# A transformer layer's prologue rearranged: quarter inputs, fewer fills, a resident bias table, another scratch layout

## The reference

```python
# setup: x (2, 1024, 128); D = 128, 16 heads of 8, F = 512; f32
def _L0_attn_ref(x, Wq, bq, Wk, bk, Wv, bv, Wo, bo, rel_emb):
    ...
    q = (x @ Wq.T + bq).reshape(b, n, h, hd).transpose(0, 2, 1, 3)   # k, v alike
    ...
    sim = jnp.einsum('bhid,bhjd->bhij', q, k)
    rp_bucket = _rel_pos_bucket_causal(n)        # 32 buckets of i - j, log spaced up to 128
    bias = rel_emb[rp_bucket]
    sim = sim + jnp.transpose(bias, (2, 0, 1)) * SCALE
    ...
    sim = sim + causal
    attn = jax.nn.softmax(sim, axis=-1)
    out = jnp.einsum('bhij,bhjd->bhid', attn, v)
    out = out.transpose(0, 2, 1, 3).reshape(b, n, d)
    return out @ Wo.T + bo

def _L0_ffn_ref(tgt, router_w, router_b, w1, b1, w2, b2, gamma, beta):
    ...
    rw = jnp.zeros_like(rw).at[..., 0].set(1.0)  # only expert 0 counts
    h = jax.nn.relu(jnp.einsum('bsd,edf->besf', tgt, w1) + b1[None, :, None, :])
    eo = jnp.einsum('besf,efd->besd', h, w2) + b2[None, :, None, :]
    tgt2 = jnp.einsum('besd,bse->bsd', eo, rw)
    x = tgt + tgt2
    ...
    return (x - mean) * jax.lax.rsqrt(var + LN_EPS) * gamma + beta

x = x + _L0_attn_ref(_layernorm(x), ...)
x = x + _L0_ffn_ref(_layernorm(x), ...)
```

## Time and profile before

| | us |
|---|---|
| median of 3 runs | 405.28 (403.5 to 411.39) |
| the profiled execution | 402.29 |
| its span on the core | 400.5 |

### The profile page before, as it was taken

The page is one execution under the profiler, slowest core; times in us unless marked ns, Lnnn a source line. Parts: engine busy times, 40 slices in busy tenths (PEclk is TensorE's granted clock), DMA queues, the critical chain, the costliest instruction groups (busy, mean ns, idle before and its releaser), DMA issues.

```text
span 400.5 us, 8158 instructions
## 1 busy us (share of the span) xinstructions
PE 321.0 (80%) x3197; PEld 153.1 (38%) x3197; DVE 287.5 (72%) x960; ACT 184.0 (46%) x258; POOL 69.5 (17%) x78
## 2 busy tenths in 40 slices
PE   0182438396999899799889979988988998999982
PEld 0131215143334335334434433443443344337752
DVE  3985356358668589588678848967875996773986
ACT  1042024131655554575565545556555545873330
POOL 9812035700001000100100100010010000161552
PEclk9996586668699999999999989999998999999998
DMA  8013422410012101201201220331222010100011
GB/s 227 26 53 116 145 90 95 148 64 3 2 43 66 39 18 52 81 1 61 75 12 44 68 64 2 86 88 26 65 79 55 15 16 12 33 2 10 5 52 53
DMA packets 18295, 21.97 MB, mean 55 GB/s; under 512 B 5584, under 2 KB 14960, under 8 KB 18256
## 3 DMA queue, kind: packets, MB, share of 16 engines
q1 hardware_dynamic: 18256, 21.45, 18.5%
HBM read 14.98 MB, written 4.23 MB: 48 GB/s over the span
## 4 chain that ended last, share of the span: by engine, by line
PE 51%; DVE 17%; DMA 15%; ACT 7%; issue 5%; SPq 4%; POOL 1%; DVEq 0%; POOLq 0%; ACTq 0%
PE ps L1015 14%; PE ps L1044 13%; PE ps L1001 13%; DMA QA<-mrow 7%; ACT PT L626 6%; PE ps L1032 5%; DMA qk_scratch<-QS 4%; DVE FM L759 3%; DVE XN L701 2%; DVE junk L766 2%; DMA KA<-qk_scratch 2%; DMA rows<-in_vectors 2%; PE ps L1077 2%; DVE st L836 1%; DVE U L889 1%
## 5 line engine op out<-in xcount | busy, mean ns | idle before, releaser
L626 ACT ACTIVATE PT<-ps 128x1024 f32<-128x1024 f32 (+1 forms) x192 | 145.8, 810 | 132.4 <-PE ps L1032 101.9
L759 DVE TENSOR_REDUCE FM<-ps 128x1 f32<-128x512 f32 (+3 forms) x176 | 108.4, 660 | 29.2 <-PE ps L1001 29.1
L1001 PE MATMUL ps<-KA,QA 96*128 96x256 bf16 (+3 forms) x544 | 108.7, 294 | 17.6 <-DMA KA<-qk_scratch 14.3
L1015 PE MATMUL ps<-QA,KA 98*128 98x512 bf16 (+3 forms) x384 | 99.0, 343 | 25.4 <-DMA QA<-mrow 10.3
L766 DVE CUSTOM_DVE_ANT_0 junk<-ps,NB 128x256 bf16<-128x256 f32 (+1 forms) x224 | 78.8, 403 | 37.3 <-PE ps L1001 37.2
L1044 PE MATMUL ps<-PT,VG 128*16 128x512 f32 (+3 forms) x768 | 86.9, 498 | 0.0
L1001 PEld LDWEIGHTS ps<-KA,QA 96*128 96x128 bf16 x544 | 44.1, 101 | 103.7 <-DVE FM L759 32.9
L1015 PEld LDWEIGHTS ps<-QA,KA 98*128 98x128 bf16 x384 | 32.5, 101 | 52.5 <-ACT PT L626 21.6
L497 POOL COPY NB<-NBH 128x1024 bf16<-128x1024 bf16 x7 | 7.3, 1040 | 212.3 <-PE ps L1044 211.4
L1032 PE MATMUL ps<-TT,flb 128*32 128x176 f16 (+4 forms) x1152 | 38.9, 245 | 0.0
L1032 PEld LDWEIGHTS ps<-TT,flb 128*32 128x32 bf16 x1152 | 21.5, 96 | 17.9 <-issue 17.0
(11 more groups left out here) (88 smaller groups left out, 255.5 us busy)
## 6 DMA issues: line engine op xcount, KB each, us to landing
QA<-qk_scratch SPq DMA_DIRECT2D x48, 96.0 KB
KA<-qk_scratch SPq DMA_DIRECT2D x16, 288.0 KB
TT<-f_scratch SPq DMA_DIRECT2D x16, 120.0 KB, 7.8
qk_scratch<-QS SPq DMA_DIRECT2D x4, 384.0 KB
qk_scratch<-QS SPq DMA_DIRECT2D x12, 128.0 KB
X<-in_x SPq DMA_DIRECT2D x2, 512.0 KB, 6.2
...
```

The lines of the kernel that those rows point to most:

```text
L626: nc.scalar.activation(PT[:, s % 3, 2 * q:2 * q + 2, off:off + w], ST[:, q, :, off:off + w], ACT.Exp).then_inc(s_exp, 1)
L759: nc.vector.tensor_reduce(FM[:, ib, heads[0]:heads[-1] + 1, piece], bank[:, 0:w * len(heads)].rearrange("p (h n) -> p h n", n=w), AX.X, AL ...
L1001: last = nc.tensor.matmul(bank[:, i * w + j - j0:i * w + j - j0 + n], QA[0:KS, p, ib // 4, h, (ib % 4) * 128:(ib % 4 + 1) * 128], KA[0:KS, ...
L1015: last = nc.tensor.matmul(ST[:, q, h % 2, off:off + w], KA[0:KST, p, jb // 4, h, (jb % 4) * 128:(jb % 4 + 1) * 128], QA[0:KST, p, ic, h, o ...
```

## The change

- **Input** in four quarters, each with its statistics and norm; `table` and `early` are issued from ScalarE's queue; `rows` has its own semaphore, and eps is a constant of VectorE's, so the first norm waits for no weights.
- **Fills**: the three of `QA` rows 64 to 96, `KA` rows 64 to 96 and `KA` rows 96 to 98 become one of `KA` rows 64 to 74 (bfloat16 ones, 8,192 elements a partition), before the loads write rows 64 to 71; the one of `junk` goes. Matmuls read 72 and 74 rows instead of 96 and 98.
- **Bias**: six small matmuls give the table with positions on partitions, [128, 3, 16]; its scratch is stored in runs of 16 elements (32 bytes) and read back in whole rows: `rev` in one load of 1 MB (8 KB a row), `TL` in two loads of 480 KB each, once, which stays in SBUF. GpSimd's new `copy_tt` makes `TT` for a group from it (960 elements a partition, reordered), in place of `load_tt`. All eight flips run ahead of the units.
- **Scratch**: K is stored as Q is, one store of 384 KB instead of three; a half is loaded in six DMAs of 24 rows, whose source begins with the 8 head elements, instead of three of 24 rows and one of 72 whose sources begin with a repeat of 3.
- **Maxima**: `move_m` is one DMA of two rows instead of two of one row.
- **Order**: the last part of Q's split for sequence 0 goes to GpSimd; units 0 to 16 come before the first scores instead of 0 to 24; ScalarE's wait for sequence 1's split ahead of the first exponentials goes, since `R` for it has another place.

```diff
-KS = 96
-MROW = 96
+KS = ROWS
+MROW = ROWS
...
-QK_AT = {3: (0, 0), 5: (0, 1), 8: (1, 0), 10: (1, 1)}
-REMAINDER_AT = {6: (0, 0), 8: (0, 1), 11: (1, 0), 13: (1, 1)}
-
-FLIP_AT = {14: 2, 15: 3, 16: 4, 18: 5, 19: 6, 20: 7}
+QK_AT = {1: (0, 0), 3: (0, 1), 5: (1, 0), 7: (1, 1)}
+REMAINDER_AT = {4: (0, 0), 6: (0, 1), 8: (1, 0), 10: (1, 1)}
+V_AT = {9: 0, 11: 1}
 RECIP_AFTER = (6, 14, 22, 30)
-OWN0 = 25
+OWN0 = 17
...
-        R = PT[:, 1:3, :, :]
-        rev = PT[:, 0, :, :].rearrange("p h n -> p (h n)").bitcast(BF16).rearrange("p (h c) -> p h c", c=256)
+        R = [PT[:, 1, :, :], OT[:, 4:6, :].rearrange("p g (c n) -> p (g c) n", n=IC)]
+        rev = PT[:, 0, :, :].rearrange("p h n -> p (h n)").bitcast(BF16)
         NUM, DEN = XN, xnT
 
         ps = ctx.enter_context(nc.psum_tensor("ps", [128, 8, 512], F32))
...
 
 
         qk_d = nc.dram_tensor("qk_scratch", (2, 2, NPART * G, HG * HD, IC), BF16, kind="Internal")
-        f16_d = nc.dram_tensor("f16_scratch", (H, 2, BW), FP16, kind="Internal")
-        fr_d = nc.dram_tensor("fr_scratch", (H, BW), BF16, kind="Internal")
-
-
-        s_x = [sem(f"s_x{b}") for b in range(B)]
-        s_w = sem("s_w")
+        f16_d = nc.dram_tensor("f16_scratch", (2, BW, H), FP16, kind="Internal")
+        fr_d = nc.dram_tensor("fr_scratch", (BW, H), BF16, kind="Internal")
...
-            for b in range(B):
-                sp.dma_start(X[:, b * TPB:(b + 1) * TPB, :], xv[:, b * TPB:(b + 1) * TPB, :]).then_inc(s_x[b], 16)
-                if b == 0:
-                    for dst, src in [(table_s[:, :], table), (early_s[:, :], early),
-                                     (rows[:, :, :], bass.AP(vectors.tensor, 0, [[0, 128], [D, 5], [1, D]]))]:
-                        sp.dma_start(dst, src).then_inc(s_w, 16)
+            for k in range(2 * B):
+                sp.dma_start(X[:, 4 * k:4 * k + 4, :], xv[:, 4 * k:4 * k + 4, :]).then_inc(s_x[k], 16)
+                if k == 1:
+                    sp.dma_start(rows[:, :, :], bass.AP(vectors.tensor, 0, [[0, 128], [D, 5], [1, D]])).then_inc(s_rows, 16)
             sp.dma_start(late_s[:, :], late).then_inc(s_late, 16)
 
             GN = HG * HD * IC
-            QN, CN = 2 * NPART * G * GN, NPART * G * GN
-
-
-            def store_q(b, c):
-
-                sp.wait_ge(s_q3[b], c * 2 + 1)
-                sp.dma_start(bass.AP(qk_d, c * CN + b * GPB * GN, [[IC, 128], [G * GN, NPART], [1, IC]]),
-                             QS[:, b, 0, :, c * IC:(c + 1) * IC]).then_inc(s_qst[b][c], 16)
-
-            def store_k(b, c):
-                sp.wait_ge(s_q3[b], c * 2 + 2)
-                for a in range(NPART):
-                    sp.dma_start(bass.AP(qk_d, QN + c * CN + (b * GPB * NPART + a) * GN,
-                                         [[NPART * GN, GPB], [IC, HG * HD], [1, IC]]),
-                                 QS[:, b, 1, a, c * IC:(c + 1) * IC]).then_inc(s_qst[b][c], 16)
+            PN = G * GN
+
+            def store(b, c, qk):
...
+                sp.wait_ge(s_q3[b][qk], c + 1)
+                sp.dma_start(bass.AP(qk_d, (2 * c + qk) * NPART * PN + b * GPB * GN, [[IC, 128], [PN, NPART], [1, IC]]),
+                             QS[:, b, qk, :, c * IC:(c + 1) * IC]).then_inc(s_qst[b][c], 16)
...
-                rows_q = [[0, NPART], [HG * IC, HD], [1, HG * IC]]
-                rows_k = [[0, NPART], [HG * IC, NPART * HD], [1, HG * IC]]
-                for a in range(NPART):
-                    sp.dma_start(QA[24 * a:24 * a + 24, p, c, :, :].rearrange("r h n -> r (h n)"),
-                                 bass.AP(qk_d, g * GN + (c * CN + a * G * GN), rows_q)).then_inc(s_ldqk[p][c], 16)
-                sp.dma_start(KA[0:ROWS, p, c, :, :].rearrange("r h n -> r (h n)"),
-                             bass.AP(qk_d, g * (NPART * GN) + (QN + c * CN), rows_k)).then_inc(s_ldqk[p][c], 16)
-
-            def load_tt(hg, p):
-                for part in range(2):
-                    sp.dma_start(TT[64 * part:64 * part + 64, p, :, :],
-                                 bass.AP(f16_d, hg * (HG * 2 * BW) + part * BW, [[1, 64], [2 * BW, HG], [1, NEARU]])
-                                 ).then_inc(s_ldt[p], 16)
+                at = g * GN + 2 * c * NPART * PN
+                rows_q = [[HG * IC, HD], [PN, NPART], [1, HG * IC]]
+                rows_k = [[HG * IC, HD], [0, NPART], [1, HG * IC]]
+                for u in range(NPART):
+                    r0 = u * NPART * HD
+                    for tile, start, pattern in ((QA, at, rows_q), (KA, at + (NPART + u) * PN, rows_k)):
+                        sp.dma_start(tile[r0:r0 + NPART * HD, p, c, :, :].rearrange("r h n -> r (h n)"),
+                                     bass.AP(qk_d, start, pattern)).then_inc(s_ldqk[p][c], 16)
 
             def move_m(p, half, g):
 
                 wait_apart(sp, s_smf, NU * g + (NU - 1 if half else UNITS.index(("m", 0))) + NSM + 1)
-                for part in range(2):
-                    sp.dma_start(QA[MROW + part:MROW + part + 1, p, half, :, :],
-                                 mrow[4 * part:4 * part + 4, half, :]).then_inc(s_md[half], 16)
+                sp.dma_start(QA[MROW:MROW + 2, p, half, :, :], mrow[:, half, :]).then_inc(s_md[half], 16)
...
-            store_q(0, 0)
-
             sp.wait_ge(s_f, 1)
-            sp.dma_start(fr_d.ap(), Fr[:, :]).then_inc(s_fst[0], 16)
-            store_k(0, 0)
+            sp.dma_start(bass.AP(fr_d, 0, [[H, 128], [128 * H, XC], [1, H]]), Fr[:, :, :]).then_inc(s_fst[0], 16)
+            sp.wait_ge(s_f, 2)
+            for part in range(2):
+                sp.dma_start(bass.AP(f16_d, part * BW * H, [[H, 128], [128 * H, XC], [1, H]]),
+                             F16[:, part, :, :]).then_inc(s_fst[1], 16)
             sp.wait_ge(s_fst[0], 16)
-            sp.dma_start(rev[:, 0:HG, :], bass.AP(fr_d, 0, [[1, 128], [BW, HG], [1, 256]])).then_inc(s_rev[0], 16)
-            sp.wait_ge(s_f, 2)
-            sp.dma_start(f16_d.ap(), F16[:, :, :]).then_inc(s_fst[1], 16)
-            sp.wait_ge(s_zero, 5)
-            sp.wait_ge(s_qst[0][0], 64)
+            sp.dma_start(rev[:, :], bass.AP(fr_d, 0, [[H, 128], [1, 256 * H]])).then_inc(s_rev, 16)
+            store(0, 0, 0)
+            store(0, 0, 1)
+            sp.wait_ge(s_fst[1], 32)
+            sp.wait_ge(s_zero, 1)
+            sp.wait_ge(s_qst[0][0], 32)
             load_half(0, 0, 0)
-            store_q(0, 1)
-            store_k(0, 1)
-            sp.dma_start(rev[:, HG:H, :], bass.AP(fr_d, HG * BW, [[1, 128], [BW, H - HG], [1, 256]])).then_inc(s_rev[1], 16)
-            sp.wait_ge(s_qst[0][1], 64)
+            for part in range(2):
+                sp.dma_start(TL[64 * part:64 * part + 64, :, :].rearrange("r u h -> r (u h)"),
+                             bass.AP(f16_d, part * BW * H, [[H, 64], [1, NEARU * H]])).then_inc(s_tl, 16)
+            store(0, 1, 0)
+            store(0, 1, 1)
+            sp.wait_ge(s_qst[0][1], 32)
             load_half(0, 0, 1)
-            sp.wait_ge(s_fst[1], 16)
-            load_tt(0, 0)
             load_half(1, 1, 0)
             load_half(1, 1, 1)
-            load_tt(1, 1)
             move_m(0, 0, 0)
...
-            for pad in (QA, KA):
-                nc.gpsimd.memset(pad[64:96, :, :, :, :].rearrange("p q c h n -> p (q c h n)").bitcast(F32),
...
+            nc.gpsimd.memset(KA[64:KST, :, :, :, :].rearrange("p q c h n -> p (q c h n)"), 1.0).then_inc(s_zero, 1)
+            pool.wait_ge(s_zero, 1)
             nc.gpsimd.memset(VG[:, :, :, :, :], 1.0).then_inc(s_zero, 1)
-            nc.gpsimd.memset(junk[:, :, :, :], 0.0).then_inc(s_zero, 1)
...
+            def copy_tt(hg, p):
+                nc.gpsimd.tensor_copy(TT[:, p, :, :].rearrange("p h u -> p u h"),
+                                      TL[:, :, bass.ds(HG * hg, HG)]).then_inc(s_tt, 1)
...
+            for c in range(2):
+                pool.wait_ge(s_mid, 2 * c + 1)
+                q = QS[:, 0, 0, :, c * IC:(c + 1) * IC]
+                nc.gpsimd.tensor_tensor(q[:, 2, :], R[0][:, 2 * c, :], q[:, 1, :], ALU.subtract).then_inc(s_q3[0][0], 1)
+            pool.wait_ge(s_zero, 2)
+            pool.wait_ge(s_rows, 16)
             add_bv(0)
             pool.wait_ge(s_v, 2)
             copy_v(0, 0)
             copy_v(1, 1)
+            pool.wait_ge(s_tl, 32)
+            copy_tt(0, 0)
+            copy_tt(1, 1)
...
                     copy_nb((2 * r + 2) % GPB + p, p)
+                    copy_tt((2 * r + 2) % GPB + p, p)
                     copy_v(g + 2, p)
...
+            act.dma_start(table_s[:, :], table).then_inc(s_tab, 16)
+            act.dma_start(early_s[:, :], early).then_inc(s_early, 16)
+            act.wait_ge(s_eps, 1)
+            nc.scalar.activation(warm[:, :], eps[:, :], ACT.Sqrt).then_inc(s_warm, 1)
...
             deviation(0)
-            turned(0)
+            turned(0, 0)
             deviation(1)
-            first_parts(0)
+            act.wait_ge(s_early, 16)
+            first_parts(0, 0)
+            turned(0, 1)
```

(71 more changed lines are left out.)

196 lines of the change are left out of this document (91 added, 105 removed).

## The result

| | before | changed |
|---|---|---|
| median (lowest to highest) | 405.43 us (403.5 to 411.39) | 393.27 us (391.6 to 393.37, 4 runs) |
| profiled span | 400.5 us | 391.5 us |
| mean granted TensorE clock | 0.924 | 0.909 |
| ratio | | 0.969, 95% interval [0.964, 0.974] |

The forecast was 368 us, with 357 to 384 as the range. The sign was right. The gain was 12 us instead of 37, and the time lies outside the range.

The account below looks back on a forecast made before the run. Start bound by transfers and their order, middle by TensorE plus a hole per group waiting for `mrow`. 400.5 - 29.2 + 3.3 - 0.65 - 9.9 = 364.0 us span, plus 1.8 is 365.8, as median 368; range 357 to 384.

Parts of the forecast that it names:

- The step that failed: Middle, GpSimd: `copy_tt` takes 2.5 us and costs nothing, as units read PSUM; at most 15 us if it blocks VectorE.
- the clock as a gain only: Rival, chance 0.12: with shorter waits TensorE's clock may hold full level, 4 us, and an earlier first half 3 more: 361.
- The start: From the fills to the first attention scores: scores start at 49.4 us instead of 78.60, a gain of 29.2.
- the fills: Start, GpSimd: two 3.5 us fills in front and the `junk` fill go; first quarter ready at 9.3 rather than 19.1.
- the leading count: `QA`/`KA` loads: engines follow the source pattern's first count, 3 before, 8 after, so 78 GB/s becomes 208.
- step 5: Start, SP's queue: second half lands at 33.5, three halves issue until 46.2, then `move_m` (0.65 + 2.57); scores at 49.4.
- Given back: First scores to second maxima: eight more units fall there, the 16.7 us stretch becomes 20, cost 3.3.
- The middle: Groups after the start: TensorE's wait for `mrow` goes, 9.9 us in six groups and 0.65 in group 0; period 31.7.
- the removed issue of `move_m`: Middle: one DMA of 8 rows instead of two of 4 removes the first issue, 0.68 us.
- The sum: Whole kernel: 400.5 - 29.2 + 3.3 - 0.65 - 9.9 = 364.0 us span, 365.8 with the 1.8 around it, median 368.
- second hole stays: Rival, chance 0.18: another engine ends TensorE's wait at step 4, so only the start counts: 375.7, as median 378.
- queued transfers: Rival, chance 0.13: at the start `TL` and `rev` loads pass ahead at half the rate; scores at 58, 377.

Follow-up runs that it names:

- the cut copy: The changed kernel with `copy_tt` of groups 2 to 7 cut to two elements, so their bias is not renewed: 365.05 us, ratio 0.899.
- the copy held: The changed kernel with `copy_tt` of groups 2 to 7 held on GpSimd until the next group's second-half maxima are done, behind `copy_v`: 365.16 us, ratio 0.900.

## Why the prediction went wrong, and where it held

**The step that failed** is the one on `copy_tt`, costed at nothing. It had two errors. The size: 2.5 us by the nearest row, measured 4.52. And the cover: I wrote that it could block VectorE and dismissed that since "the units read PSUM". They do, and they were not blocked; the cut copy shows that the rest of it costs nothing. But between the units stand the few small instructions that make the maxima, a cast from SBUF to SBUF and a subtraction with two inputs from SBUF. I had checked the many instructions and not the one in the chain. The place could be read before: the new copy is queued right behind `NB`, whose copy ended at 128.04, and the cast came 1.3 us later.

```profile
129.36 0.17 DVE L780 CAST MC<-NM 128x16 bf16<-128x16 f32 x1
```

Even the 2.5 us copy of the forecast, from 128.0 on, would have reached over it, though by my estimate only to 130.5. The bound that I gave it, 15 us, is near the size of the holes alone (16) by chance: it is six times a copy of 2.5, and the holes are six times what is left of a copy of 4.52. The clock behind them (12 us) was in no case of mine; I had the clock as a gain only.

**The start held**, nearly term by term: first quarter 8.8 (forecast 9.3), K out at 17.2 (18.0), K's store landed 19.8 (21.5), first unit 29.3 (28.5), second half's store waited for until 33.0 (33.5), first scores 48.5 (49.4). The gain there is 30.1 for 29.2. Its grounds held as well: the fills (6 us when put back) and the leading count (the loads at 0.19 again when it is 3). The rate that I took for the new loads, 0.5 at 200 GB/s, was not reached: 0.40 at 126. SP's issues, 0.65 us each (forecast 0.70), allow little more, so the size of that term was not put to a test. The issue of `move_m` that step 5 takes at 0.65 us stands as 0.68 in the earlier trace rows; here it took 0.69.

**Given back** was mis-sized. The stretch from the first scores to the second maxima is 23.2 us, not 20, against 16.7. VectorE is 14.7 us busy in it and TensorE 19.8, 5.0 and 5.6 more, both about as forecast (5.4 and up to 5). But I let them overlap. The chain above has VectorE from 64.96 to 70.81 (3.68 us of reductions, then the `junk` units); TensorE is 3.1 us busy in these 5.9 and ends with 2.2 us of waiting for it. No run tests this term by itself.

**The middle held, once the copy is out of the way**: the wait for `mrow` went from TensorE's list, and the period with the copy held is 31.75 for a forecast of 31.7, TensorE 30.66 busy. From the second send on, that kernel needs 226.9 us where before needed 240.7, 13.8 less against 10.6 forecast. The 3.2 us more are luck in part: the undisturbed periods give 1.6 each, as forecast, but two of before's were 35.5 and 36.0 us long, its clock down to 0.75 and 0.66 for some 5 us (from 235 and from 305), and with the copy held no such stretch is left in the middle. One of the forecast's terms was empty: the removed issue of `move_m` is worth nothing.

**The sum**: with the copy held, 400.5 - 23.5 - 13.8 = 363.2 us of span, for a forecast of 364.0, where the larger gain in the middle makes up for what was given back. Of the rivals, neither "second hole stays" (378) nor "queued transfers" (377) is what happened. A second hole did stay, but another one: the first was cured, and the copy put its own in the same place.
